# An accumulating DMA for the first of four additions over the 16 states of a state-space scan, with two state tiles, and a changed order of the softmax transposes, LayerNorm rows and decays, in a one-core fp32 transformer-like layer

## The reference

```python
x = x + cross_attention(layernorm(x), ctx, mask)   # x: 64 x 32 x 512, ctx: 64 x 257 x 512, 16 heads of 32
x = x + mamba(layernorm(x))                        # d_inner 1024, 16 states, 4 taps
x = x + ffn_uint8(layernorm(x))                    # 512 -> 2048 -> 512, fake quantisation
# inside mamba, for every inner channel d, state n and position l (h = 0 at l = 0):
dt = softplus(bcd[..., -1:] * dt_w + dt_b)
h[n] = exp(dt * A[n]) * h[n] + dt * xs * B[n]
y    = sum over n of h[n] * C[n]   + xs * D
out  = (y * silu(z)) @ Wout
```

## Time and profile before

| | us |
|---|---|
| median of 3 runs | 2366.3 (2363.32 to 2367.36) |
| the profiled execution's own time | 2362.47 |
| its span | 2360.7 |
| VectorE (DVE) busy | 2020.6 |
| TensorE (PE) busy | 1942.2 |
| ScalarE (ACT) busy | 1676.1 |
| GpSimd (POOL) busy | 344.0 |

### The profile page before, as it was taken

One profiled execution on the slowest core, in us unless ns is written; L12 is line 12 of the kernel. 1 busy time (PEld: TensorE's weight loads), 2 busy tenths in 40 slices (PEclk: granted clock), 3 DMA queues, 4 the chain that ended last, 5 costly groups with the idle time before them and its releaser, 6 DMA issues.

```text
span 2360.7 us, 36464 instructions
## 1 busy us (share of the span) xinstructions
PE 1942.2 (82%) x11244; PEld 1371.5 (58%) x11244; DVE 2020.6 (86%) x2429; ACT 1676.1 (71%) x4598; POOL 344.0 (15%) x296
## 2 busy tenths in 40 slices
PE   6998898989798888989898989798888987430678
PEld 5676566666575666666666666575656665320233
DVE  1534989999999999999999999999999999899577
ACT  2457787877878787778787877878887878653391
POOL 1000121121211111111111111212111111000003
PEclk9999998989999999989999989999999998765789
DMA  7521010111111101112121211111111211210113
GB/s 224 221 74 65 25 66 26 64 37 60 41 55 39 46 37 36 64 37 64 34 66 25 64 37 60 41 60 34 48 36 35 64 32 42 77 42 22 56 37 120
DMA packets 81206, 136.48 MB, mean 58 GB/s; under 512 B 17408, under 2 KB 40592, under 8 KB 75920
## 3 DMA queue, kind: packets, MB, share of 16 engines
q1 hardware_dynamic: 81040, 134.89, 17.8%
HBM read 117.69 MB, written 17.18 MB: 57 GB/s over the span
## 4 chain that ended last, share of the span: by engine, by line
DVE 31%; ACT 23%; PE 15%; issue 12%; DMA 3%; POOL 2%; DVEq 1%; ACTq 0%; SPq 0%; POOLq 0%
ACT dA L1141 10%; DVE hb L1446 10%; PE bank L874 6%; DVE hb L1457 5%; DVE hb L1451 5%; DVE hb L1442 3%; PE bank L944 2%; PE bank L784 2%; DVE xs L1407 2%; DMA BC<-bcd_dram 2%; ACT Pr L1012 2%; ACT Pr L1045 2%; PE bank L954 1%; ACT KT L990 1%; DVE dt L1415 1%
## 5 line engine op out<-in xcount | busy, mean ns | idle before, releaser
L1141 ACT ACTIVATE dA<-dt,A_sb 128x124 f32<-128x124 f32 x2048 | 610.6, 390 | 91.7 <-DVE dt L1421 58.6
L1446 DVE TENSOR_TENSOR_SCAN hb<-dA,hb 128x2048 f32<-128x2048 f32 x128 | 566.1, 4423 | 21.4 <-ACT dA L1141 17.1
L775 PE MATMUL bank<-ctxT,wk_sb 128*128 128x256 f32 x2048 | 489.1, 398 | 65.3 <-ACT ctxT L982 62.8
L775 PEld LDWEIGHTS bank<-ctxT,wk_sb 128*128 128x128 f32 x2048 | 403.2, 200 | 139.2 <-ACT ctxT L982 60.4
L784 PE MATMUL bank<-wv_sb,ctxT 128*128 128x512 f32 x1024 | 462.1, 594 | 0.9 <-ACT ctxT L982 0.9
L1457 DVE TENSOR_TENSOR hb<-hb 128x1024 f32<-128x1024 f32 (+2 forms) x384 | 301.8, 786 | 12.2
L1451 DVE TENSOR_TENSOR hb<-hb,BC 128x2048 f32<-128x2048 f32 x128 | 296.9, 2319 | 6.3 <-issue 3.4
L874 PE MATMUL bank<-xn2T,win_sb 128*128 128x128 f32 x2048 | 269.5, 299 | 36.0 <-ACT xn2T L1070 31.7
L784 PEld LDWEIGHTS bank<-wv_sb,ctxT 128*128 128x128 f32 x1024 | 186.4, 191 | 193.8 <-issue 192.5
L1442 DVE TENSOR_TENSOR hb<-u,BC 128x2048 f32<-128x2048 f32 x128 | 293.2, 2291 | 3.4
L874 PEld LDWEIGHTS bank<-xn2T,win_sb 128*128 128x128 f32 x2048 | 266.2, 215 | 41.6 <-ACT xn2T L1070 36.2
(11 more groups left out here) (131 smaller groups left out, 2357.6 us busy)
## 6 DMA issues: line engine op xcount, KB each, us to landing
ctx_sb<-in_ctx_dram SPq DMA_DIRECT2D x64, 512.0 KB, 3.7
BC<-bcd_dram SPq DMA_DIRECT2D x32, 1024.0 KB, 4.9
maskb<-in_mask_Bx1x1xS_fk_dram SPq DMA_DIRECT2D x64, 128.5 KB, 3.3
wstage<-in_L_ffn_w_dram SPq DMA_DIRECT2D x4, 2048.0 KB, 10.6
x_sb<-in_x_dram SPq DMA_DIRECT2D x16, 256.0 KB, 3.4
win_sb<-in_L_attn_in_proj_w_dram SPq DMA_DIRECT2D x1, 4096.0 KB, 25.2
bo_sb<-bias_dram SPq DMA_DIRECT2D x64, 64.0 KB, 2.1
x_dram<-x SPq DMA_DIRECT2D x16, 256.0 KB, 2.1
```

Source lines behind the costliest of these rows:

```text
L775: last = pe.matmul(bank[6 + j][:, (m % 2) * KF:(m % 2 + 1) * KF], wk_sb[:, c, m * P:(m + 1) * P], ctxT[:, c, :], start=(c == 0), stop=(c = ...
L1141: last = act.activation(dA[:, c % 2, n * BT:(n + 1) * BT, 1:], dt[:, c, :].rearrange("p (b s) -> p b s", s=S)[:, :, 1:], ACT.Exp, scale=A_ ...
L1446: ins = dve.tensor_tensor_scan(flat, dA[:, c % 2].rearrange("p n s -> p (n s)"), flat, 0.0, ALU.mult, ALU.add)
```

## The change

For chains 0 to 6 the first addition of the tree (1024 elements for each partition) leaves VectorE: when C is done, GpSimd issues a DMA that adds the upper eight states of the tile to its lower eight, SBUF to SBUF. VectorE waits for that DMA and does the additions of 512 and 256 and the last one. Chain 7 keeps its whole tree on VectorE. `hb` becomes two tiles, one for even and one for odd chains, and the order of the steps becomes M(c) S(c) T(c-1) C(c). 32 steps remain; the table CHAIN holds their order. Batch b1 now has steps 22 to 26: C(5), M(6), S(6), T(5), C(6).

`ln_out` becomes one 512-column buffer with waits for its other readers, `apart` goes, and two short-lived uses of ln_out move to x1 and x2. In the order of the calls: `mamba_rows` comes after `normalise`; in b0 the transposes of P (and ScalarE's copies of them) come between `mamba_transpose` and `mamba_in`; `mamba_skip` moves from b2 to b3; a half chain of decays, (4,1), moves from the end of b3 to b0's place "m", where it is the next interval's work. `ffn_prefetch` moves into the last interval and waits for S(7) of the last tile.

```diff
-        ln_out = sb("ln_out", [P, 3, D])
+        ln_out = sb("ln_out", [P, D])
...
-        sb("apart", [P, 800])
-        hb = sb("hb", [P, NS, P])
+        hb = sb("hb", [P, 2, NS, P])
...
+        CHAIN = [(0, 0), (0, 1), (0, 2)]
+        for c in range(1, IC):
+            CHAIN += [(c, 0), (c, 1), (c - 1, 3), (c, 2)]
+        CHAIN.append((IC - 1, 3))
+        DONE = {step: k + 1 for k, step in enumerate(CHAIN)}
-        FINISH = {(0, "a"): range(14, 15), (0, "b"): range(15, 17), (0, "c"): range(17, 21), (0, "e"): range(21, 22),
-                  (1, "a"): range(22, 23), (1, "b"): range(23, 25), (1, "c"): range(25, 27), (1, "d"): range(27, 28),
-                  (2, "a"): range(28, 29), (2, "b"): range(29, 31), (2, "c"): range(31, 32)}
-        BEGIN = {(2, "w"): range(0, 1), (2, "d"): range(1, 2), (2, "e"): range(2, 4), (3, "a"): range(4, 5),
-                 (3, "b"): range(5, 7), (3, "c"): range(7, 9), (3, "d"): range(9, 11), (3, "e"): range(11, 14)}
+        FINISH = {(0, "a"): range(14, 15), (0, "b"): range(15, 16), (0, "c"): range(16, 20), (0, "e"): range(20, 22),
+                  (1, "a"): range(22, 23), (1, "b"): range(23, 24), (1, "c"): range(24, 26), (1, "d"): range(26, 27),
+                  (2, "a"): range(27, 28), (2, "b"): range(28, 31), (2, "c"): range(31, 32)}
+        BEGIN = {(2, "w"): range(0, 1), (2, "d"): range(1, 2), (2, "e"): range(2, 3), (3, "a"): range(3, 4),
+                 (3, "b"): range(4, 6), (3, "c"): range(6, 8), (3, "d"): range(8, 10), (3, "e"): range(10, 14)}
-        FINISH_DECAYS = {(0, "t"): ((5, 0), (5, 1)), (0, "w"): ((6, 0),), (1, "m"): ((6, 1),),
+        FINISH_DECAYS = {(0, "m"): ((4, 1),), (0, "t"): ((5, 0), (5, 1)), (0, "w"): ((6, 0),), (1, "m"): ((6, 1),),
-                        (3, "w"): ((3, 0), (3, 1)), (3, "e"): ((4, 0), (4, 1))}
+                        (3, "w"): ((3, 0), (3, 1)), (3, "e"): ((4, 0),)}
...
-                    if b == 0 and front:
-                        part.mamba_rows(tm)
...
                     if here:
                         part.normalise(g)
+                    if b == 0 and front:
+                        part.mamba_rows(tm)
...
                         part.mamba_transpose(tm, keys)
+                    if b == 0 and here:
+                        part.transpose_p(g)
+                    if b == 0 and front:
                         part.mamba_in(tm, keys)
...
-                    if here:
+                    if b > 0 and here:
                         part.transpose_p(g)
...
+                    if b == 3 and front:
+                        part.mamba_skip(tm)
...
-                    if b == 2 and front:
-                        part.mamba_skip(tm)
...
@@ GpSimd
+                def scans(self, t, steps):
+                    for k in steps:
+                        c, op = CHAIN[k]
+                        if op == 2 and not whole(c):
+                            pool.wait_ge(scan_step, 4 * IC * t + k + 1)
+                            apart(pool)
+                            pool.dma_start(hb[:, c % 2, 0:NS // 2, :], hb[:, c % 2, NS // 2:NS, :], accum_op=ALU.add
+                                           ).then_inc(hb_added, 16)
@@ VectorE, the tree
+                            dve.wait_ge(scan_step, 4 * IC * t + DONE[c, 2])
+                            if not whole(c):
+                                dve.wait_ge(hb_added, 16 * ((IC - 1) * t + c + 1))
+                            n = NS // 2 if whole(c) else NS // 4
+                            done = (2 * IC + 1) * t + 2 * c
+                            while n > 1:
+                                dve.tensor_tensor(tile[:, 0:n, :], tile[:, 0:n, :], tile[:, n:2 * n, :], ALU.add
+                                                  ).then_inc(sum_step, 1)
+                                done += 1
+                                dve.wait_ge(sum_step, done)
+                                n //= 2
+                            ins = dve.tensor_tensor(u[:, c, :], tile[:, 0, :], tile[:, 1, :], ALU.add)
```

More of the change, by code:

```diff
@@ L448, in interval @@
                         part.mamba_bcd(tm, keys)
+                    if b == 2 and back and not front:
+                        part.ffn_prefetch()
                     if b == 2 and back:
@@ L549, in ungrouped, with tiles, whole @@
             return wstage[1][:, first + c * D:first + (c + 1) * D].rearrange("p (m j d) -> p m j d", m=DC, d=DEPTH)
+        def tiles(n):
+            return min(n, NT) if isinstance(n, int) else n
+        def whole(c):
+            return c == IC - 1
         def apart(engine):
@@ L730, in _ @@
             for c in range(DC):
-                last = pe.transpose(bank[0][:, c * B:(c + 1) * B], ln_out[0:B, 0, c * P:(c + 1) * P], idf[0:B, 0:B])
+                last = pe.transpose(bank[0][:, c * B:(c + 1) * B], ln_out[0:B, c * P:(c + 1) * P], idf[0:B, 0:B])
             last.then_inc(lastT_psum, 1)
@@ L842, in q_transpose @@
                     for c in range(DC):
-                        last = pe.transpose(bank[0][:, c * P:(c + 1) * P], ln_out[:, 0, c * P:(c + 1) * P], idf[:])
+                        last = pe.transpose(bank[0][:, c * P:(c + 1) * P], ln_out[:, c * P:(c + 1) * P], idf[:])
                     last.then_inc(xnT_psum, 1)
@@ L866, in mamba_transpose @@
                     for c in range(DC):
-                        last = pe.transpose(bank[6][:, c * P:(c + 1) * P], ln_out[:, 1, c * P:(c + 1) * P], idf[:])
+                        last = pe.transpose(bank[6][:, c * P:(c + 1) * P], ln_out[:, c * P:(c + 1) * P], idf[:])
                     last.then_inc(xn2T_psum, 1)
@@ L931, in out_transpose @@
                     for c in range(DC):
-                        last = pe.transpose(bank[6][:, c * P:(c + 1) * P], ln_out[:, 2, c * P:(c + 1) * P], idf[:])
+                        last = pe.transpose(bank[6][:, c * P:(c + 1) * P], ln_out[:, c * P:(c + 1) * P], idf[:])
                     last.then_inc(xn3T_psum, 1)
@@ L1013, in softmax, with layernorm_rows @@
                                        accum_out=soft[:, 1, m:m + 1]).then_inc(exp_done, 1)
-                def layernorm_rows(self, i, t, rows, used):
+                def layernorm_rows(self, i, t, rows):
                     act.wait_ge(ln_rstd[i], 3 * (t + 1))
-                    wait(act, used, t)
-                    act.activation(ln_out[:, i, :], rows, ACT.Identity, scale=stats[:, i, 9:10],
+                    act.activation(ln_out[:], rows, ACT.Identity, scale=stats[:, i, 9:10],
                                    bias=stats[:, i, 10:11]).then_inc(ln_done[i], 1)
                 def ln_q_rows(self, t):
-                    self.layernorm_rows(0, t, x_sb[:], xnT_psum)
+                    wait(act, xn2T_psum, t - 1)
+                    self.layernorm_rows(0, t, x_sb[:])
                 def mamba_rows(self, t):
```

74 lines of the change are left out of this document (40 added, 34 removed).

## The result

The changed kernel takes **2477.68 us** (median; 2474.93 to 2479.31), the kernel before 2364.81 beside it: a ratio of 1.0476, 95% interval 1.0457 to 1.0494. It is slower by 113 us. I had forecast 2286 us with a range of 2232 to 2366, so the result lies outside the range and on the other side.

What follows compares the result with a forecast made beforehand. VectorE bounds the kernel, with TensorE setting b1's end. An interval loses 4.0 us in the rest and 0.6 in b1, to 121.3; 14 intervals -64, tail -11, start -5, together -80: 2286 us, range 2232 to 2366.

Steps and rivals of the forecast that it cites:

- The step that failed: b0: the last LayerNorm factor comes 6.8 us after the scores, the in-projection can start at 9.3.
- T(3): b0: its DMA lands 1.7 us late, within the 2.1 us convolution wait, so it costs nothing.
- T(5)'s wait in b1: b1: late by about 1 us, inside the new 3.4 us of VectorE idle time.
- The rival that was nearest, C: DMA issue held behind VectorE's M, landing at 8.5 us, waits in b3: 2376 us; chance 18%.
- b1: Scores to scores: TensorE sets the end, 0.6 us saved from 20.0, about 3.4 us VectorE idle before b2's scores.
- My last sentence: An interval of 125 us or more with landings under 6.7 us would make the account of b1 wrong.
- The convolution's wait: b0: VectorE waits 2.1 us for the in-projection instead of 1.1, 1.0 us lost an interval.
- The exp's wait in b3: b3: VectorE's wait for the softmax exp grows from 1.52 to 1.9 us, 0.4 lost an interval.
- b3's waits of T on the DMA: b3: none at T(1) and T(2), since 6.7 us of cover exceeds the landing by 0.5 us.
- The DMA's landing: Each accumulating DMA: 6.2 us, from a 1 MB store at 5.7 us plus 0.5 for slower issue.
- The early transposes of P: b0: they lie inside the wait for the copy, letting the in-projection start at 9.3 us; no further gain priced.
- Start and tail: Outside the 14 intervals: 5 us gained in the first interval with a front, 11 us after the last convolution wait.

Runs made afterwards that it cites:

- e4: The changed kernel without the accumulating DMA for chains 3 and 5 (their trees wholly on VectorE): 2438.65 us, ratio 1.0314 to the kernel before.
- e8: The changed kernel with one empty semaphore increment more for each chain on VectorE, layout alone: 2411.3 us, ratio 1.0206 to the kernel before.
- e7: The changed kernel with chain 6's accumulating DMA issued only after the step-size row has landed: 2442.96 us, ratio 1.0332 to the kernel before.
- e2: The changed kernel with LayerNorm factors split: VectorE adds epsilon and negates the mean, GpSimd only takes the power, ScalarE the product: 2302.94 us.
- e1: The changed kernel with T(2), the last step of an interval, moved behind b0's statistics: 2329.47 us, ratio 0.9854 to the kernel before.
- e14: The kernel of e2 with b0's transposes of P back behind the in-projection: 2344.65 us, ratio 0.9918 to the kernel before.
- e13: The kernel of e2 without any accumulating DMA, all eight trees whole on VectorE: 2391.04 us, ratio 1.0116 to the kernel before.
- the split: The edit of e2, LayerNorm factors shared among VectorE, GpSimd and ScalarE; 2303 us against 2411 for e8, its match in layout.

## Why the prediction was wrong

**The step that failed** is the one that set b0: "That path starts with POOL's last LayerNorm factor, 6.8 us after the scores began". I took that number over from the trace of before. It isn't a property of GpSimd but of what VectorE does beside it, and the change took exactly those short additions away. In the changed kernel it is 11.5 us (1218.21 against 1206.68). Everything behind it in b0 moved by that: the in-projection, not at 9.3 but at 15.2; the issue of C(3)'s DMA; T(3), late by 5.12 us where I had 1.7. T(5)'s wait in b1 grew in the same way, 4.91 instead of "about 1". What cost time was the row and the in-projection, not the waits of T: without the DMA of chain 3 the convolution starts hardly earlier (e4). The two rows that showed it stood in my own evidence: 2.05 us under a two-input instruction, 0.22 just ahead of one.

**The rival that was nearest, C, had the right cause and the wrong victim.** It let VectorE's M hold back the DMA's issue. The issue took 0.90 us on average (101.0 us for 112), also under M, and landings took 4.7. What was held back were the instructions ahead of it in GpSimd's queue. The Trainium skill (SBUF — State Buffer, Who interferes with whom) was right on both: two-input VectorE instructions hold GpSimd's reads, and descriptor writing isn't held by them. By that page the factors, which read SBUF, were the ones to price anew, and I applied it to the DMA alone. The scan behaves here as a two-input instruction too: it held L1212 to its end.

**What the prediction did not see.** The loop's edge: 4.0 us an interval before x1 and more of the 1.25 us before the scores, 66 us in all (e8). The prediction spoke of the 1.25 us as VectorE's largest wait there and never asked what "issue" stood for, nor what had covered the rest. The step-size row: 35 us (e7), as a consequence of the late T(5); I looked at what the DMA's queue does to GpSimd's order, not to SyncE's small transfers.

**Term by term**, in e2, where both are out of the way, against my account of an interval:

- *b1*: forecast 19.4 us from scores to scores (20.0 - 0.6), e2 has 19.5 (19.8 in the mean of ten intervals), with 4.24 us of VectorE idle before b2's scores where I had 3.4. In the changed kernel 21.1, and T(5)'s wait is not the cause. The two stretches below are b1 of the changed kernel and b1 of e8; in both T(5) waits 4.9 us. The granted clock differs, 0.92 and 1.00:

```profile
1107.43:1128.56 21.13, 19.49 (x113) 12.60 (x112) 14.78 (x19) 18.20 (x49) 10.37 (x6) 0.92 0.17 36
```

```profile
1072.56:1092.48 19.92, 18.28 (x118) 12.10 (x116) 14.69 (x18) 18.55 (x51) 9.85 (x5) 1.00 0.18 36
```

  e1 says the same from the other side: 21.15 us at a clock of 0.92 (1158.96 to 1180.11) with 0.15 us of waiting at T(5). So TensorE set the end of b1, as forecast, and what the forecast left out was its clock. My last sentence, that an interval of 125 or more with quick landings would make the account of b1 wrong, was itself wrong: the most of it was the loop's edge and b0.
- *The convolution's wait*: forecast 2.1, e2 2.37 and the changed kernel 2.21, there with the whole of b0 later. Right in size, though the changed kernel reached it on another way.
- *The exp's wait in b3*: forecast 1.9, e2 2.54, the changed kernel 2.53.
- *b3's waits of T on the DMA*: none, as forecast.
- *The DMA's landing*: 6.2 forecast, 4.7 measured. The Trainium skill's figure (DMA: Bandwidth & Descriptors, Anatomy of one DMA), an estimate of 4.4, was nearer than my 6.2 from other transfers.
- *Not in the sum*: the scans' wait for decays. 17.1 us in all before, 40.2 us in e2, 1.6 an interval more. VectorE, with shorter trees, overtakes ScalarE in b3.

```profile
DVE hb L1498 <- ACT dA L1167: 40.2, 30, 4.9
```

With 0.6 from the exp that is 2.2 us, against the 2.0 us between e2's 123.3 and my 121.3; that the two agree so well is partly luck, since e2 also has gains that the sum did not hold, such as the earlier LayerNorm row. The early transposes of P were priced at nothing beyond the start of the in-projection; e14 shows 42 us.

- *Start and tail*: to the first x1 e2 gained 7.0 us (249.6 against 256.6) where I had 5, the changed kernel 3.7. From the last x1 to the end of the last gating e2 gained 12.1 (162.4 against 174.5) where I had 11, although two waits of T on the DMA lie there, 4.9 us together; the changed kernel gained 5.8 (168.7).

So the sum of VectorE's own work was about right (the DMA is worth 88 us in e13), and the error was to treat the durations of a small engine and of the loop's edge as constants.

**What stays open.** How the 108 us of the split divide between the late LayerNorm row and the late DMA wasn't tried by itself; by e4's trace the waits of T are the small part (0.4 us an interval in b0, at most 0.8 in b1), and the step-size row 1.9 to 2.0. Why TensorE's clock in b1 was lower in some kernels than in others isn't shown either. Why exactly these layouts need 5 packets fewer for a jump wasn't tried either; only this one padding was.

## What to carry to other kernels

Before reordering a busy engine, look at every tiny instruction of an engine that shares a resource with it, and price it by what will run beside it after the change, not by its row of before. Put critical little work where its neighbour has gaps, or give it to another engine. A wait marked "issue" at a loop's head is worth a look at the instruction queue's packets: here eight empty instructions a tile moved the time by 66 us, so two kernels should be compared with equal packet counts before a difference is put down to their content.

## What the runs showed of the hardware

- A GpSimd instruction on 128 words took 0.27 us alone and up to 3.98 us under a scan, held to the scan's end; three in a row were held by three VectorE instructions in turn. Where GpSimd's first began 0.04 us ahead of a two-input VectorE instruction, it took 0.23 us. A GpSimd addition that began first made a VectorE multiplication 0.8 us longer.
- An accumulating DMA within SBUF (512 KB added onto 512 KB) was issued in 0.90 us and landed 4.7 us after; 3.5 us instead of 1.5 passed between the issue of a small store and that of the load that waits for it, when the DMA had been issued 1.5 us ahead of the store.
- The loop's backward jump cost VectorE 5.9 us a pass at 138 instruction packets, 0.4 at 83. What stands last in the loop decides how much is seen: behind a scan of 4.42 us, in the kernel before, only 1.25 us were left.
- TensorE ran the same 16 products in 6.38 us after 5.08 us of idleness (granted clock 0.58) and in 3.72 after 1.46 (1.00); the transposes of P ahead of the in-projection took the low clock on themselves (0.80 to 0.96 for the in-projection).
